# Centring the weights instead of the rows in a two-layer graph network on one core

## The reference

```python
# layer 0
H   = (adj != 0);  w = adj[:, 0, :]
Dn  = 1 / (H @ w);  Be = 1 / H.sum(axis=1)               # guarded against zero
conv(x, W, b) = Dn * (H @ (Be * (H.T @ (x @ W.T)))) + b
h   = layer_norm(relu(conv(x, W1, b1))) * gamma + beta   # 512 wide
x   = LN(x + (conv(h, W2, b2) + x))                      # 256 wide
# layer 1
agg = (adj @ x) / adj.sum(-1)
x   = LN(x + relu(concat([x, agg]) @ WL.T))
```

## Time and profile before

| what | value |
|---|---|
| median of the three runs | 1118.35 us |
| profiled execution | 1120.11 us |
| its span | 1118.3 us |
| busy: PE, VectorE, ScalarE, GpSimd | 1095.7, 700.8, 322.2, 185.9 us |
| granted TensorE clock, mean | 0.997 |
| share of the chain that ended last: PE, DMA | 95%, 2% |

### The profile page before, as it was taken

How to read it: one execution, slowest core, us unless ns; L and a number is a source line. 1 busy time by engine, 2 the same in 40 slices (tenths; PEclk the granted TensorE clock), 3 DMA queues, 4 the chain that set the end, 5 groups by cost and what they waited for, 6 DMA issues and landing times.

```text
span 1118.3 us, 18768 instructions
## 1 busy us (share of the span) xinstructions
PE 1095.7 (98%) x6112; PEld 899.9 (80%) x6112; DVE 700.8 (63%) x1846; ACT 322.2 (29%) x712; POOL 185.9 (17%) x256
## 2 busy tenths in 40 slices
PE   5899999999999999999999999999999999999997
PEld 5769789697887969779697887969789697886966
DVE  4754866646856659557685486854867647756326
ACT  4433311433024221242213331133312433024230
POOL 0501204020041200412012110311204011041000
PEclk9999999999999999999999999999999999999999
DMA  9405442075220671206621246114452164300001
GB/s 223 107 6 117 104 102 70 6 150 116 62 66 0 150 150 38 56 18 132 150 56 38 63 102 145 47 38 100 109 110 55 20 145 107 76 10 1 1 1 38
DMA packets 65032, 86.18 MB, mean 77 GB/s; under 512 B 9457, under 2 KB 55153, under 8 KB 65009
## 3 DMA queue, kind: packets, MB, share of 16 engines
q1 hardware_dynamic: 65008, 85.89, 34.7%
HBM read 77.47 MB, written 8.39 MB: 77 GB/s over the span
## 4 chain that ended last, share of the span: by engine, by line
PE 95%; DMA 2%; SPq 1%; DVE 1%; issue 0%; ACT 0%; DVEq 0%; ACTq 0%
PE bank L705 41%; PE bank L771 11%; PE bank L733 10%; PE bank L809 10%; PE bank L831 10%; PE bank L793 10%; PE bank L801 3%; DMA raw<-in_adj_dram 2%; PE bank L817 1%; SPq L241 1%; DVE HT L511 0%; SPq L253 0%; DVE H L461 0%; ACT adjT L376 0%; DVE xres L493 0%
## 5 line engine op out<-in xcount | busy, mean ns | idle before, releaser
L705 PE MATMUL bank<-yv,adjT 128*128 128x257 f32 x1024 | 223.3, 379 | 0.0
L705 PEld LDWEIGHTS bank<-yv,adjT 128*128 128x128 f32 x1024 | 193.6, 189 | 31.7 <-issue 3.8
L368 ACT ACTIVATE small<-mv,small 128x1 f32<-128x1 f32 x192 | 56.6, 295 | 362.0 <-DVE mv L499 266.4
L733 PE MATMUL bank<-x_hi,H 128*128 128x258 f32 x512 | 123.0, 288 | 4.7 <-DVE m_lo L504 2.4
L705 PE MATMUL bank<-x_hi,H 128*128 128x256 f32 x512 | 122.6, 283 | 0.0
L705 PE MATMUL bank<-m_hi,HT 128*128 128x256 f32 x512 | 121.6, 280 | 0.0
L705 PE MATMUL bank<-x_lo,H 128*128 128x256 f32 x512 | 121.1, 280 | 0.0
L318 POOL TENSOR_TENSOR xres<-x_in 128x256 f32<-128x256 f32 x64 | 46.7, 763 | 447.4 <-DMA out_dram<-xres 412.3
L705 PE MATMUL bank<-m_lo,HT 128*128 128x256 f32 x512 | 120.9, 279 | 0.0
L504 DVE SCALAR_TENSOR_TENSOR m_lo<-bank,small,m_hi 128x256 fp32r<-128x256 f32 x128 | 61.1, 483 | 94.7 <-ACT m_hi L363 94.7
L793 PE MATMUL bank<-W1T,zT 128*128 128x512 f32 x256 | 120.3, 592 | 0.0
(11 more groups left out here) (78 smaller groups left out, 1635.4 us busy)
## 6 DMA issues: line engine op xcount, KB each, us to landing
raw<-in_adj_dram SPq DMA_DIRECT2D x128, 256.0 KB, 9.1
adjB<-in_adj_dram SPq DMA_DIRECT2D x224, 128.0 KB, 3.5
x_in<-in_x_dram SPq DMA_DIRECT2D x32, 256.0 KB, 4.6
out_dram<-xres SPq DMA_DIRECT2D x128, 64.0 KB, 1.6
w_row<-in_adj_dram SPq DMA_DIRECT2D x8, 512.0 KB, 3.7
W2n<-in_L_gnn_W_dram SPq DMA_DIRECT2D x1, 512.0 KB, 4.1
W1n<-in_L_gnn_W_dram SPq DMA_DIRECT2D x1, 512.0 KB, 8.0
WLn<-in_L_gnn_W_dram SPq DMA_DIRECT2D x1, 512.0 KB, 9.2
```

What stands on the lines that cost most here:

```text
L368: nc.scalar.activation(std[:, i:i + 1], mv[:, which, i, 1:2], ACT.Sqrt, bias=eps_c)\
L705: last = mm(bank(stage, i)[:, 0:n_cols], lhsT, rhs, start=(k == 0 and part == 0), stop=(k == NT - 1 and part == parts - 1))
L733: last = mm(*args, start=(c == 0 and n == 0), stop=(c == NT - 1 and n == 1))
```

## The change

The mean of a row need not be subtracted from the row if every output column of the weight behind it sums to zero over the index of the row; and the factor 1/std of a row can be applied to the product. So W2 * gamma, and each half of WL, are centred once in the setup over that index. Rows go into TH and TX as they are, Q is scaled by rstd_h as VectorE drains it, V by rstd_1 as ScalarE drains it. x1 itself, which the last residual needs normalized, is normalized by ScalarE in place after the V drains. LAG_T goes from 3 to 1 and LAG_Q from 4 to 2. In the setup gamma and beta are loaded as rows broadcast to all partitions, W2 comes first in the queue, and beta @ W2.T is a row sum on VectorE, spread by two matmuls with the identity.

```diff
-LAG_T = 3
-LAG_Q = 4
+LAG_T = 1
+LAG_Q = 2
...
-            sp.dma_start(gamma_c, gamma.rearrange("(k p) -> p k", p=P), allow_slow_non_contiguous=True)\
-              .then_inc(rows_loaded, 16)
-            sp.dma_start(beta_c, beta.rearrange("(k p) -> p k", p=P), allow_slow_non_contiguous=True)\
-              .then_inc(rows_loaded, 16)
             sp.dma_start(W2n[:, :, :], W2.rearrange("(t p) d -> p t d", p=P)).then_inc(W2_loaded, 16)
+            sp.dma_start(gamma_row[:, :], gamma.partition_broadcast(P)).then_inc(rows_loaded, 16)
+            sp.dma_start(beta_row[:, :], beta.partition_broadcast(P)).then_inc(rows_loaded, 16)
             load_x(0)
...
-                    empties_bank(nc.scalar.activation(yv[:, i, 0:2 * D], bank("V", i)[:, :], ACT.Copy), "V", i)
+                    act.wait_ge(rstd_done["1"], b * NT + i + 1)
+                    empties_bank(nc.scalar.activation(yv[:, i, 0:2 * D], bank("V", i)[:, :], ACT.Identity,
+                                                      scale=rstd_1[:, i:i + 1]), "V", i)
                     if i + 2 < NT:
                         take_x1T(i + 2)
+                act.wait_ge(neg_mean_done, b + 1)
+                for i in range(NT):
+                    nc.scalar.activation(xres[:, i, :], xres[:, i, :], ACT.Identity, scale=rstd_1[:, i:i + 1],
+                                         bias=neg_mean_1[:, i:i + 1]).then_inc(normed["1"], 1)
...
+            dve.wait_ge(W2_loaded, 16)
             dve.wait_ge(rows_loaded, 16 * 2)
-            for k in range(NH):
-                nc.vector.tensor_copy(beta_wide[:, k, :], beta_c[:, k:k + 1].to_broadcast([P, P]))\
-                  .then_inc(beta_wide_done, 1)
...
+                nc.vector.scalar_tensor_tensor(out=W2b[:, :], in0=W2n[:, o, :], scalar=1.0, in1=beta_row[:, :],
+                                               op0=ALU.mult, op1=ALU.mult, accum_out=bW2_c[:, o:o + 1])\
+                  .then_inc(W2_part, 1)
...
+                nc.vector.tensor_tensor(W2n[:, o, :], W2n[:, o, :], gamma_row[:, :], ALU.mult).then_inc(W2_part, 1)
...
+            def take_means(parts, done):
+                for n, part in enumerate(parts):
+                    nc.vector.bn_stats(stats[:, 0, n, :], part)
+                dve.drain()
+                for n, part in enumerate(parts):
+                    nc.vector.bn_aggr(mv[:, 0, n, :], stats[:, 0, n, :])
+                dve.drain()
+                for n, part in enumerate(parts):
+                    nc.vector.tensor_scalar(part, part, mv[:, 0, n, 0:1], None, ALU.subtract).then_inc(done, 1)
...
+            take_means([W2n[:, o, :] for o in range(ND)], W2_centred)
...
+            take_means([WLn[:, o, side * D:(side + 1) * D] for o in range(ND) for side in range(2)], WL_centred)
...
                         inverse_root("h", std_h, rstd_h, s - 1, b)
-                        centre("h", 0, hrow[:, (s - 1) % H_SLOTS, :], rstd_h, s - 1, b)
...
-                        empties_bank(nc.vector.tensor_tensor(q_f32[:, i % 2, :], bank("Q", i)[:, 0:D],
-                                                             bW2_row[:, :], ALU.add), "Q", i)
+                        dve.wait_ge(rstd_done["h"], b * NT + i + 1)
+                        empties_bank(nc.vector.scalar_tensor_tensor(
+                            out=q_f32[:, i % 2, :], in0=bank("Q", i)[:, 0:D], scalar=rstd_h[:, i:i + 1],
+                            in1=bW2_row[:, :], op0=ALU.mult, op1=ALU.add), "Q", i)
...
-                        centre("1", 1, xres[:, i - 1, :], rstd_1, i - 1, b)
...
+                        dve.wait_ge(normed["1"], b * NT + i + 1)
                         nc.vector.scalar_tensor_tensor(out=xres[:, i, :], in0=o_f32[:, i % 2, :], scalar=0.0,
...
-                    for k in range(NH):
-                        last = mm(banks[0][:, 0:D], beta_wide[:, k, :], W2T[:, k, :],
-                                  start=(k == 0), stop=(k == NH - 1))
+                    for o in range(ND):
+                        last = mm(banks[0][:, o * P:(o + 1) * P], bW2_wide[:, o, :], ident[:, :],
+                                  start=True, stop=True)
...
-                        pe.wait_ge(normed["h"], b * NT + i + 1)
+                        pe.wait_ge(relu_done, b * NT + i + 1)
...
-                    pe.wait_ge(normed["1"], b * NT + i + 1)
+                    pe.wait_ge(*emptied("S4", i, b))
```

More of the change, by code:

```diff
@@ L152, in graph_net @@
         WLn, _, nxt = place("WLn", [P, ND, 2 * D], F32, nxt)
-        W2T, _, nxt = place("W2T", [P, NH, D], F32, nxt)
-        beta_wide, _, _ = place("beta_wide", [P, NH, P], F32, nxt)
+        gamma_row, _, nxt = place("gamma_row", [P, DH], F32, nxt)
+        beta_row, _, nxt = place("beta_row", [P, DH], F32, nxt)
+        W2b, _, nxt = place("W2b", [P, DH], F32, nxt)
+        bW2_wide, _, _ = place("bW2_wide", [P, ND, P], F32, nxt)
         def col(n):
@@ L159, in graph_net @@
         (dn, dn_pos, dn_safe, dn_inv, rDn, be_safe, rBe, deg_safe, rdeg, std_h, rstd_h, std_1, rstd_1,
-         std_o, rstd_o, gb) = (col(n) for n in range(16))
-        gamma_c, beta_c, eps_c = gb[:, 0:NH], gb[:, NH:2 * NH], small[:, 16, 0:1]
+         std_o, rstd_o, neg_mean_1) = (col(n) for n in range(16))
+        eps_c, bW2_c = small[:, 16, 0:1], small[:, 18, 0:ND]
         stats, _, _ = place("stats", [P, 3, NT, 6], F32)
         mv, _, _ = place("mv", [P, 3, NT, 2], F32)
-        assert NT >= 2 * NH and at[0] <= nc.sbuf_usable_end, (at[0], nc.sbuf_usable_end)
+        assert at[0] <= nc.sbuf_usable_end, (at[0], nc.sbuf_usable_end)
         banks = [ctx.enter_context(nc.psum_tensor(f"bank{n}", [P, 512], F32)) for n in range(N_BANKS)]
@@ L191, in graph_net @@
         norms = ("h", "1", "o")
+        neg_mean_done = sem("neg_mean_done")
         stats_done = sem("stats_done")
@@ L195, in graph_net @@
         rstd_done = {n: sem(f"rstd_done_{n}") for n in norms}
-        normed = {n: sem(f"normed_{n}") for n in norms}
-        W2T_scaled, beta_wide_done = sem("W2T_scaled"), sem("beta_wide_done")
+        normed = {n: sem(f"normed_{n}") for n in ("1", "o")}
+        W2_part, W2_centred, WL_centred, bW2_wide_done = (
+            sem(n) for n in ("W2_part", "W2_centred", "WL_centred", "bW2_wide_done"))
         out_stored = sem("out_stored")
@@ L346, in split_x_hi @@
                 nc.scalar.activation(x_hi[:, :, 0:D], x_in[:, :, :], ACT.Copy).then_inc(x_hi_done, 1)
-            targets = [W2T[:, 2 * k:2 * k + 2, :].rearrange("p k o -> p (k o)") for k in range(NH // 2)] + \
+            targets = [gW2T[:, 2 * k:2 * k + 2, :].rearrange("p k o -> p (k o)") for k in range(NH // 2)] + \
                       [W1T[:, d, :] for d in range(ND)] + \
@@ L621, in graph @@
                         nc.vector.bn_aggr(mv[:, 1, i, :], stats[:, 1, i, :]).then_inc(var_done["1"], 1)
+                dve.wait_ge(var_done["1"], b * NT + NT)
+                dve.wait_ge(rstd_done["1"], b * NT + NT)
+                nc.vector.scalar_tensor_tensor(out=neg_mean_1, in0=mv[:, 1, :, 0], scalar=-1.0, in1=rstd_1,
+                                               op0=ALU.mult, op1=ALU.mult).then_inc(neg_mean_done, 1)
                 nc.vector.memset(yv[:, :, 2 * D:YP], 1.0).then_inc(y_ones, 1)
@@ L677, in _ @@
                      for d in range(ND)]
-            loads = (W2_loaded, W1_loaded, WL_loaded)
+            loads = ((W2_centred, ND), (W1_loaded, 16), (WL_centred, 2 * ND))
             for n, four in enumerate(fours):
@@ L681, in _ @@
                 if n % 2 == 0:
-                    pe.wait_ge(loads[n // 2], 16)
+                    pe.wait_ge(*loads[n // 2])
                 if n >= 2:
```

23 lines of the change are left out of this document (12 added, 11 removed).

## The result

The changed kernel takes 1123.89 us (median of 6 runs, 1122.94 to 1125.54), the kernel before on the same chip 1119.13 us (6 runs): the ratio is 1.0044, 95% interval 1.0031 to 1.0057. It is slower by 4.8 us, outside the forecast range. The profiled execution of the changed kernel took 1124.23 us, with a span of 1122.4 us: 4.1 us more than before, by either measure.

The account below looks back on a forecast made before the run. PE, busy for 98% of the span, was taken to bound the kernel. Only the setup's load queue added time, +0.7 us, all other terms being 0: from the median 1118.35 to 1119.0 us, range 1117.0 to 1121.0.

Parts of the forecast that it names:

- The split: Whole kernel: the change can act only through the setup, +0.7 us, or through a PE wait in the loop, 0.
- The setup: the load queue: Setup loads ahead of adj: two added rows cost 1.7 us, earlier W2 gains 1.06; +0.7 us, bounds -0.1 and +2.3.
- The setup: VectorE: VectorE's weight work and first H in the setup: some 2 us later but hidden; term 0, bounds 0 and +1.5.
- no idle time between parts 2 and 4: Sign in the setup: the forecast is wrong if VectorE has no idle time between these parts of adj.
- Rival 3: Setup: VectorE is 3 us later than worked out, 1.2 come through, 1120.2 us; chance 0.09.
- rival 1: Clock behind the setup: PE's wait shrinks and the 1.2 GHz stretch may go, -1.7 us, 1117.3; chance 0.12.
- The loop: what is removed: VectorE passes taken out of the loop: worth nothing, as PE never waited for them; term 0.
- The loop: what becomes tight: Chains to TH and Q at lags 1 and 2: tightest margin 0.2 us; waits 0, bounds 0 and 0.8 us.
- Rival 2: Between Q(6) and Q(7): PE waits in every graph, 8 times the excess, 1122.2 us at 0.4 excess; chance 0.09.
- ScalarE behind V: Eight added passes over `xres` per graph, 0.42 to 0.58 us each: hidden by 1.2 to 2.5 us; term 0.

Follow-up runs that it names:

- e4: Changed kernel without the two row loads, gamma taken as 1 and beta as 0, set by VectorE: 1117.87 us, ratio 0.9995.
- e5: Kernel before plus 0.5 MB of setup loads behind W2, as two loads of 128 different 2 KB rows: 1120.92 us, ratio 1.0018.
- e10: Kernel before plus 0.5 MB in the setup behind W2, as one 4 KB row broadcast to all partitions: 1121.14 us, ratio 1.0019.
- e3: Kernel before plus the change's two broadcast row loads (gamma, beta) behind W2, unused: 1123.48 us, ratio 1.0036.
- e9: Kernel before with the two bias rows loaded only when part 4 of adj has landed: 1116.53 us, ratio 0.9979.
- e6: Changed kernel with gamma and beta loaded once to one partition and spread by two PE matmuls: 1121.85 us, ratio 1.0023 to the kernel before.
- e2: Changed kernel with twenty small instructions added in VectorE's setup, shifting its later code: 1121.36 us, ratio 1.0020 to the kernel before.
- e7: e6 with LAG_T 2, LAG_Q 3 and bias rows loaded only after part 4 of adj: 1118.83 us, ratio 0.9998 to the kernel before.
- e8: e7 with x's high part ahead of the W2 copies on ScalarE, and gamma and beta read from PSUM: 1115.65 us, ratio 0.9971 to the kernel before.

## Why the prediction was wrong, step by step

**The split held, the sizes did not.** The change could act through the setup or through a wait in the loop, the prediction said, and gave +0.7 and 0. It was +1.8 (3.3 less 1.5) and +2.3 in the profiled executions.

**The setup: the load queue. This step failed.** "1.7 - 1.06 = +0.7 us, bounds -0.1 and +2.3". The gain of 1.06 is there (e4: 34.61 for 35.60), and the price of 0.5 MB is about right for two other kinds of 0.5 MB (e5 1.0, e10 2.0 us). But the price of these two loads is 4.4 us (e3). It was taken per MB from loads that were thought of the same kind: WL is no broadcast at all, `w_row` is one row of 4 KB, which e10 shows to be cheaper, and the 1.30 us of the two bias rows, from which the 3.4 us per MB came, were mostly not theirs (e9: 0.5). The term measured +3.3, 1 us above the upper bound.

**The setup: VectorE. Its term of 0 came out, but by luck.** The pieces came out as worked out: 5.5 us for W2 (8.07 to 13.58) for 5.5, 3.0 for WL for 3.4; but the rows landed 1.5 us later than taken and WL at 17.4 instead of 14.7, so H(0) began at 23.45 instead of 21.3, behind a wait of 3.85 us for WL. The two tiles before part 2 were done at 27.6 instead of 25.0, off by 2.6, more than the 1.8 that the prediction allowed; it cost nothing because part 2 was later still. VectorE then caught up at part 2, where it waited 1.76 us (0.6 in the prediction). It did not meet a wait ahead of part 4, because part 2 had come 4.4 us late: the sign named for "no idle time between parts 2 and 4" did appear. Rival 3, VectorE late, was no cause here but stood right behind: e6, which took the load away, ran into it.

**The clock (rival 1, chance 0.12). It came true, but not for its reason**, -1.5 us for the 1.7 worked out. Its reason was that the wait shrinks; the reason given against it, that the wait keeps its length, held (2.4 us in both), and yet the low stretch was gone. So the wait's length alone does not decide, and as far as the runs show it was chance. Among the kernels here with a wait of 2.3 to 2.4 us, the clock fell behind it in before, e2, e6 and e10, and did not in after, e3, e4, e5 and e7. The Trainium skill (TensorE: Matmul & The Clock Gate, The HAM clock gate) has the clock low after an idle window; behind waits of this length the traces show both levels, so that statement does not decide the case. The times of e6 fall into two clusters, 1120.35 to 1120.54 and 1121.79 to 1121.92, 1.5 us apart: the size of this term. That its being there or not is what separates them is argued, not shown.

**The loop: what is removed.** Held: 43 us less on VectorE (the prediction had about 60) are worth nothing. e2 has a period of 134.60 against 134.58.

**The loop: what becomes tight. This step failed, in its bounds.** "Term for waits: 0, bounds 0 and 0.8"; measured +2.3. The chain to Q(7) was worked out right (times from the start of P(7)): relu at 2.70 us (2.71 in the prediction), the statistics at 3.37 (3.37). Then comes the gap. bn_aggr and all behind it are 0.43 us late: the drain of Q(5) at 4.75 (4.32), the copy of TH(7) at 5.59 (5.16), its end at 6.17, and the weight load at 6.28 where 5.9 was wanted. Rival 2 had the place, the price ("8 times the excess") and the point from which it decides; it had a chance of 0.09, because each of its delays was taken as measured. The margin of 0.2 us was measured against operations alone, in a kernel whose loop has no instruction loads. The changed kernel has stalls of 0.3 to 0.5 us at two places of each pass, which appear as "issue" in its waits; the bounds had no room for one. The drain of Q with a factor was 0.06 us longer, as taken (0.48 for 0.42). Q(1), Q(6) and TH(7) by itself showed no wait.

**ScalarE behind V.** Held:

```profile
279.33 4.03 ACT L454 ACTIVATE xres<-xres,small 128x256 f32<-128x256 f32 x8
```

Eight passes with a bias take 4.03 us in a row, 0.50 each, between the 0.42 and 0.58 that bounded it. The estimate of 0.51 from the Trainium skill (ScalarE: Activation LUTs, Rules for kernel authors) is near this pace; one pass by itself lasts 0.59 us in the trace, and the passes overlap. The drain of V with a scale takes 0.69 us instead of the 0.60 taken from the earlier trace rows. VectorE has no row of waiting for these passes.

**The chances.** Two cases that were weighed at 0.12 and 0.09 came together, with a load term beyond its bound. The range, 1117 to 1121, had left out the middle of rival 2, and its upper end stood on a bound read from loads of another kind.

## What to carry to other kernels

Price a new load by a load of the same shape in the same place, and if the trace has none, bound it widely: the same 0.5 MB cost 1.0, 2.0 or 4.4 us in the traces here. Where instructions of several engines are set close together, leave a margin above the stalls that the profile books as "issue", 0.5 us here, or one more tile of distance, which cost nothing here (e7, period 134.58). Compare the count of instruction loads of the two kernels, in the loop above all: it went from 0 to 27 between 200 and 1000 us, and no row of the kernel before could have shown its stalls. And ask of each load what its landing starts elsewhere: the bias rows, needed by nobody yet, let GpSimd loose on the stretch in which VectorE sets the end; holding them back gained 2.2 us (e9), the mended change on top of it 0.9 (e8).
